# Hyperedge degrees taken from accumulating comparisons on VectorE instead of from products with ones, and the high parts of the second aggregation ahead of its low parts

## The reference, cut to what matters

```python
H = (adj != 0).astype(x.dtype)
w = adj.reshape(N, -1)[:, :C]
xw = jnp.einsum('ncd,hd->nch', x, W)
Dn = jnp.einsum('nce,ne->nc', H, w);  Dn = jnp.where(Dn > 0, 1.0 / Dn, 0.0)
Be = H.sum(axis=1);                   Be = jnp.where(Be > 0, 1.0 / Be, 0.0)
m = Be[:, :, None] * jnp.einsum('nce,nch->neh', H, xw)
out = Dn[:, :, None] * jnp.einsum('nce,neh->nch', H, m)
```

## Time and profile before

| | |
|---|---|
| median of three runs | 738.5 us (737.72 to 739.07) |
| the profiled execution, its own time | 737.89 us |
| its span, first to last instruction | 736.4 us |
| granted TensorE clock, mean | 0.987 |
| PE busy | 697.6 us (95%), 5573 products |
| DVE busy | 637.7 us (87%) |
| ACT busy | 495.6 us (67%) |
| POOL busy | 298.5 us (41%) |
| one graph in the steady loop | about 42.5 us |

### The profile page before, as it was taken

One profiled execution on the slowest core, in us unless ns is written; L12 is line 12 of the kernel. 1 busy time (PEld: TensorE's weight loads), 2 busy tenths in 40 slices (PEclk: granted clock), 3 DMA queues, 4 the chain that ended last, 5 costly groups with the idle time before them and its releaser, 6 DMA issues.

```text
span 736.4 us, 16435 instructions
## 1 busy us (share of the span) xinstructions
PE 697.6 (95%) x5573; PEld 486.5 (66%) x5573; DVE 637.7 (87%) x1569; ACT 495.6 (67%) x971; POOL 298.5 (41%) x685
## 2 busy tenths in 40 slices
PE   4787999999999999999999999999999999999983
PEld 2365595866758586776858577685957668595772
DVE  3887799889989898998989999898998989898676
ACT  4565858667595857668594866859486685957563
POOL 4142524245352524435352434436243543624233
PEclk9999999999999999999999999999999999999997
DMA  8447449376665839476573947556493756537312
GB/s 285 181 76 240 99 131 229 59 232 134 214 129 151 200 58 267 103 219 123 167 175 73 273 81 228 114 194 148 101 259 67 234 116 202 110 89 161 58 31 57
DMA packets 42591, 111.73 MB, mean 152 GB/s; under 512 B 4160, under 2 KB 5312, under 8 KB 42560
## 3 DMA queue, kind: packets, MB, share of 16 engines
q0 software_dynamic: 13536, 41.42, 31.8%
q1 hardware_dynamic: 29024, 69.92, 27.3%
HBM read 69.91 MB, written 16.25 MB: 117 GB/s over the span
## 4 chain that ended last, share of the span: by engine, by line
PE 86%; DVE 6%; ACT 3%; DMA 1%; issue 1%; POOL 1%; SPq 0%; POOLq 0%; DVEq 0%; ACTq 0%
PE bank L1278 16%; PE bank L1279 16%; PE bank L1280 16%; PE bank L1363 7%; PE bank L1364 7%; PE bank L1422 4%; PE bank L1423 4%; PE bank L1392 3%; PE bank L1332 3%; PE bank L1394 3%; PE bank L1380 2%; PE bank L1325 2%; DMA b1b<-b 1%; PE bank L1435 1%; PE bank L1410 1%
## 5 line engine op out<-in xcount | busy, mean ns | idle before, releaser
L1278 PE MATMUL bank<-xth,ewh 128*128 128x512 f16 (+1 forms) x272 | 101.0, 371 | 2.5 <-DVE ewl L794 2.5
L1279 PE MATMUL bank<-xtl,ewh 128*128 128x512 f16 (+1 forms) x272 | 101.0, 371 | 0.0
L1280 PE MATMUL bank<-xth,ewl 128*128 128x512 f16 (+1 forms) x272 | 100.8, 371 | 0.0
L519 ACT ACTIVATE silu<-bank,ebcol,ksc 128x512 f32<-128x512 f32 x120 | 90.5, 769 | 9.2 <-POOL comb L389 4.9
L1278 PE MATMUL bank<-w2h,hnth 128*128 128x256 f16 x256 | 70.3, 275 | 0.2 <-issue 0.2
L1279 PE MATMUL bank<-w2l,hnth 128*128 128x256 f16 x256 | 70.3, 275 | 0.0
L1280 PE MATMUL bank<-w2h,hntl 128*128 128x256 f16 x256 | 70.2, 274 | 0.0
L560 ACT ACTIVATE a1h<-bank,be 128x256 f16<-128x256 f32 x64 | 26.9, 470 | 55.7 <-PE bank L1423 52.5
L893 DVE SCALAR_TENSOR_TENSOR hntl<-bank,hnth 128x512 f16<-128x512 f32 x64 | 42.7, 687 | 23.5 <-ACT hnth L537 23.5
L666 ACT ACTIVATE uh<-bank,be 128x256 f16<-128x256 f32 x64 | 26.9, 471 | 53.7 <-PE bank L1364 53.7
L1422 PE MATMUL bank<-xsh,h 128*128 128x256 f16 x256 | 59.3, 280 | 1.1 <-DVE xsl L776 1.1
(11 more groups left out here) (260 smaller groups left out, 2124.9 us busy)
## 6 DMA issues: line engine op xcount, KB each, us to landing
adjin<-adj SPq DMA_DIRECT2D x16, 1024.0 KB, 5.3
adjtin<-adjt SPq DMA_DIRECT2D x16, 1024.0 KB, 7.9
xin<-x SPq DMA_DIRECT2D x16, 512.0 KB, 7.0
xb<-xn SPq DMA_DIRECT2D x16, 512.0 KB, 4.0
xb<-x POOLq DMA_DIRECT2D x16, 512.0 KB, 8.7
xb<-b POOLq DMA_DIRECT2D x16, 512.0 KB, 5.4
xb<-vadd POOLq DMA_DIRECT2D x16, 512.0 KB, 4.5
out<-x SPq DMA_DIRECT2D x15, 512.0 KB, 4.9
```

The source lines that it names most:

```text
L519: af(silu[:, i % 4, :], bank[E_BANK[i]][:, :], ACT.Silu, bias=ebcol[:, i:i + 1], scale=ksc[:, 2:3]).then_inc(silu_dn, 1)
L1278: mm(outp, lh, rh, start=first, stop=False)
L1279: mm(outp, lh, rl, start=False, stop=False)
L1280: return mm(outp, ll, rh, start=False, stop=last)
```

## The change

The degrees are no longer products. `prep_ht` makes `ht16` tile by tile, and each of the four comparisons also adds up its row into a column of `deg` (`accum_out`). The first two tiles are compared early, ahead of `hnt_part(g, 0)`, and the other two where all four were. `degrees` moves to the end of the body of the graph before, behind `prep_h`, and `be` gets two buffers. `dna` and `dnb` move from DVE to POOL (`scale_dn`), where they stand ahead of `prep_x`. In `a2_half` all products with `a1h` come first and wait for ACT only; `turned_x2(f, 0)` moves in between them and those with `a1l`. The semaphore counts follow.

```diff
@@ POOL
+            def scale_dn(g):
+                gp.wait_ge(d_step, 4 * g + 4)
+                tt(dna[:, :], dn[:, :], ksc[:, 0:1].to_broadcast([P, CT]), ALU.mult).then_inc(dn_scaled, 1)
+                tt(dnb[:, :], dn[:, :], ksc[:, 1:2].to_broadcast([P, CT]), ALU.mult).then_inc(dn_scaled, 1)
...
+                if conv:
+                    if not ffn:
+                        gp.wait_ge(b_scale, 1)
+                    scale_dn(g)
                 if prep and ffn:
                     prep_x(g + 1)
@@ DVE
-            def prep_ht(g, odd):
-                dve.wait_ge(adjt_in, 16 * g + 16)
-                TS(ht16[odd][:, :, :], adjtin[:, :, :], 0.0, None, ALU.not_equal).then_inc(ht_made, 1)
+            def prep_ht(g, odd, tiles=range(CT)):
+                if tiles[0] == 0:
+                    dve.wait_ge(adjt_in, 16 * g + 16)
+                for t in tiles:
+                    TS(ht16[odd][:, t, :], adjtin[:, t, :], 0.0, None, ALU.not_equal, ALU.add,
+                       accum_out=deg[:, t:t + 1]).then_inc(ht_made, 1)
...
-                dve.wait_ge(d_step, 6 * g + 4)
-                TS(dna[:, :], dn[:, :], ksc[:, 0:1], None, ALU.mult).then_inc(d_step, 1)
+                dve.wait_ge(d_step, 4 * g + 4)
...
-            def degrees(g):
-
-                dve.wait_ge(deg_rdy, g + 1)
-                TS(dmax[:, :], bank[DEG_BANK][:, DEG], 1.0, None, ALU.max).then_inc(be_max, 1)
+            def degrees(g, odd):
+
+                dve.wait_ge(ht_made, 4 * g + 4)
+                TS(dmax[:, :], deg[:, :], 1.0, None, ALU.max).then_inc(be_max, 1)
                 dve.wait_ge(be_max, g + 1)
-                v.reciprocal(be[:, :], dmax[:, :]).then_inc(be_dn, 1)
+                v.reciprocal(be[odd][:, :], dmax[:, :]).then_inc(be_dn, 1)
...
                     x1_half(f, 1, late)
-                if conv:
-                    degrees(g)
                 if ffn:
                     stats_x1(f, 1)
                 if conv:
                     if not ffn:
                         prep_ht(0, 0)
+                        degrees(0, 0)
...
-                    TS(dnb[:, :], dn[:, :], ksc[:, 1:2], None, ALU.mult).then_inc(d_step, 1)
...
                 if ffn:
                     combine(f, 1)
+                if prep:
+                    prep_ht(g + 1, 1 - odd, (0, 1))
                 if conv and ffn:
                     hnt_part(g, 0)
...
                 if prep:
-                    prep_ht(g + 1, 1 - odd)
+                    prep_ht(g + 1, 1 - odd, (2, 3))
...
                 if prep:
                     prep_h(g + 1)
+                    degrees(g + 1, 1 - odd)
@@ PE
-                pe.wait_ge(a1_lo, 4 * g + CG * half + CG)
+                def part(a, first, last):
+                    for d in range(KD):
+                        for k in range(CG * half, CG * half + CG):
+                            ins = mm(bank[A2_BANK[d]][:, :], a[:, k, P * d:P * d + P], ht16[odd][:, k, :],
+                                     start=(first and k == 0), stop=(last and k == CT - 1))
+                        if last and half == 1:
+                            ins.then_inc(a2_rdy, 1)
+
+                pe.wait_ge(a1_hi, 4 * g + CG * half + CG)
                 if half == 0 and ffn:
                     pe.wait_ge(u_lo, 4 * g)
                     pe.wait_ge(x1_dn, 4 * (g - 1) + 2)
...
+                part(a1h, True, False)
+                if ffn and half == 0:
+                    turned_x2(g - 1, 0)
+                pe.wait_ge(a1_lo, 4 * g + CG * half + CG)
+                part(a1l, False, True)
...
-                    for e in range(CT):
-                        for k in range(CT):
-                            ins = mm(bank[DEG_BANK][:, DEG][:, e:e + 1], h16[:, k, P * e:P * e + P], one16[:, :],
-                                     start=(k == 0), stop=(k == CT - 1))
-                    ins.then_inc(deg_rdy, 1)
-
...
-                if ffn:
-                    turned_x2(f, 0)
```

More of the change, by code:

```diff
@@ L128, in build @@
         xb = sb("xb", [P, CT, D], F32)
-        dmax, be = (sb(n, [P, CT], F32) for n in ("dmax", "be"))
+        deg, dmax = sb("deg", [P, CT], F32), sb("dmax", [P, CT], F32)
+        be = (sb("be_even", [P, CT], F32), sb("be_odd", [P, CT], F32))
         dsum, dclip, drec, dn, dna, dnb = (sb(n, [P, CT], F32) for n in ("dsum", "dclip", "drec", "dn", "dna", "dnb"))
@@ L203, in build @@
         a2_lo, v_lo, xt_lo, ct_lo, y_dn = (sem(n) for n in ("a2_lo", "v_lo", "xt_lo", "ct_lo", "y_dn"))
+        dn_scaled = sem("dn_scaled")
         comb_st, half_sum = sem("comb_st"), sem("half_sum")
@@ L306, in _ @@
             nc.gpsimd.memset(m16[:, :, :], 0.0).then_inc(tables, 1)
-            nc.gpsimd.memset(one16[:, :], 1.0).then_inc(tables, 1)
-            gp.wait_ge(tables, 13)
+            gp.wait_ge(tables, 12)
             for m in (ident16, ident):
@@ L572, in body @@
                 if conv:
-                    a1_part(act, g, 0)
+                    a1_part(act, g, odd, 0)
                 if ffn:
@@ L576, in body @@
                 if conv:
-                    a1_part(act, g, 1)
+                    a1_part(act, g, odd, 1)
                 if conv and not ffn:
@@ L821, in setup_mag_b @@
             def setup_mag_b():
-                dve.wait_ge(tables, 16)
+                dve.wait_ge(tables, 15)
                 dve.wait_ge(b_abs, KH + 1)
@@ L912, in y_part, with a1_part @@
                     ALU.mult, ALU.add).then_inc(y_dn, 1)
-            def a1_part(g, j):
+            def a1_part(g, odd, j):
                 dve.wait_ge(a1_hi, 4 * g + CG * j + CG)
                 for e in range(CG * j, CG * j + CG):
-                    STT(a1l[:, e, :], bank[A1_BANK[j]][:, D * (e % CG):D * (e % CG) + D], be[:, e:e + 1], a1h[:, e, :],
+                    STT(a1l[:, e, :], bank[A1_BANK[j]][:, D * (e % CG):D * (e % CG) + D], be[odd][:, e:e + 1], a1h[:, e, :],
                         ALU.mult, ALU.subtract).then_inc(a1_lo, 1)
@@ L983, in x1_half @@
                     dve.wait_ge(xb_dn, 16 * g + 16)
-                    dve.wait_ge(d_step, 6 * g + 6)
+                    dve.wait_ge(dn_scaled, 2 * g + 2)
                     if again:
@@ L1026, in body @@
                 if conv:
-                    a1_part(g, 0)
+                    a1_part(g, odd, 0)
                 if late:
@@ L1032, in body @@
                         setup_scale_a()
-                    a1_part(g, 1)
+                    a1_part(g, odd, 1)
                 if late:
@@ L1068, in body @@
                         d_vector(g)
-                    dve.wait_ge(d_step, 6 * g + 5)
+                    dve.wait_ge(dn_scaled, 2 * g + 1)
                     z_part(g, 0)
@@ L1389, in a2_half @@
                     pe.wait_ge(x1_dn, 4 * (g - 1) + 2)
-                for d in range(KD):
-                    for k in range(CG * half, CG * half + CG):
-                        mm(bank[A2_BANK[d]][:, :], a1h[:, k, P * d:P * d + P], ht16[odd][:, k, :],
-                           start=(k == 0), stop=False)
-                        ins = mm(bank[A2_BANK[d]][:, :], a1l[:, k, P * d:P * d + P], ht16[odd][:, k, :],
-                                 start=False, stop=(k == CT - 1))
-                    if half == 1:
-                        ins.then_inc(a2_rdy, 1)
+                part(a1h, True, False)
[3 more added lines that the diff above has]
+                part(a1l, False, True)
             def body(pe, g, odd, conv, ffn, late, prep):
@@ L1427, in body @@
                             turn_mags(a_mag, slice(W1, W1 + 1), 0, a_turn)
-                    pe.wait_ge(ht_made, g + 1)
+                    pe.wait_ge(ht_made, 4 * g + 4)
                     pe.wait_ge(w_cur, g + 1)
@@ L1608, in tail @@
                 last_out(1)
-            pe.wait_ge(tables, 18)
+            pe.wait_ge(tables, 17)
             steps(pe, body, tail)
```

24 lines of the change are left out of this document (11 added, 13 removed).

## The result

The changed kernel takes 733.79 us (median of six runs, 732.65 to 735.57) against 738.79 us for the kernel before in six runs; the ratio is 0.9931, with a 95% interval of 0.9908 to 0.9954. The forecast was 733.6 us, and 731.6 to 736.8 us. The profiled execution took 732.65 us with a span of 731.1 us, 5.3 us less than the span before.

What follows compares the result with a forecast made beforehand. PE's instruction list was taken to set the period from the second graph on; -5.7 us for the degree products and +0.8 us in the first two graphs gave -4.9, from 738.5 to 733.6 us, range 731.6 to 736.8 us.

Steps and rivals of the forecast that it cites:

- PE loses the degree products: On PE ahead of A1: 16 products leave its list, 0.41 us a graph over 14 graphs, 5.7 us.
- A comparison costs 0.65 us: On DVE: each accumulating comparison takes 0.65 us a tile, 2.6 us a graph instead of 1.13.
- The far bound (0.80): Upper cost of a comparison on DVE: the hntl distance of 0.60 plus an accumulator read of 0.20 us; total time 734.6 us.
- The early pair hides in the hole: On DVE ahead of hntl of tile 0: two comparisons, 1.3 us, fit an idle stretch of 1.45 us.
- ctl is next, with 0.10 us: If the early pair overran, ctl for out_product would be late; an overrun over 0.10 us a graph stalls PE.
- The late pair is hidden: On DVE ahead of ul: 1.3 us replaces 1.13, ul starts 0.17 us late, and nothing passes on to PE.
- Moved: degrees, dna and dnb at new places: a1l keeps 0.1 us, x2 ends 0.14 us late, no stall on PE.
- rival A: At a1l and x2: chains without slack give back half of the 0.41 us; 736.4 us; chance 0.16.
- B: Rival: the early pair overruns the hole, DVE bounds through ctl, out_product stalls each graph; up to 746.5 us; chance 0.08.
- The reorder of a2_half costs and brings nothing: Second aggregation on PE: x2 gets 0.86 us more, a2_rdy of the first bank comes 0.43 us later; both costed at nothing.
- The start, +0.8 us: First two graphs: early pair ahead of hntl +1.0, dna's trip to POOL +0.1, be off the chain -0.3 us.
- The rest, 0: Behind the first transposed_h of graph 15: a change of 0 us was forecast.

Runs made afterwards that it cites:

- e2_no_products: The kernel before with the 16 degree products left out and be made from a constant; 732.16 us, ratio 0.9918.
- e1_deg_first: The changed kernel with degrees one place earlier, ahead of prep_h and behind the second pair of comparisons; 733.15 us, ratio 0.9928 to the kernel before.
- the repeat: The changed kernel itself run once more, with no edit; 734.01 us, ratio 0.9945 to the kernel before.
- e8_pair_at_jump: The kernel before with two short, unused four-column DVE instructions behind prep_h at the end of each body; 739.88 us, ratio 1.0016.
- e7_dna_on_vector: The changed kernel with dna and dnb scaled on DVE again, at their old places; 734.12 us, ratio 0.9937 to the kernel before.
- e9_best: The changed kernel with degrees ahead of prep_h and, in graph 0, all four comparisons at the late place; 731.90 us, ratio 0.9911 to the kernel before.

## Why the prediction was right, and the step that failed

- *PE loses the degree products, 0.41 us a graph.* Right: 0.40 us with the products alone left out (e2_no_products), and 42.05 us in every body without a jump.
- *A comparison costs 0.65 us.* 0.61 us, at the 0.60 of the `hntl` row that I leaned on. The far bound (0.80) had the accumulator's read at its full length, but the next comparison starts with it.
- *The early pair hides in the hole; ctl is next, with 0.10 us.* Right in the place: the hole keeps 0.37 us, and an overrun of 0.235 us makes PE wait for `ctl`. The slack of 0.10 us was not confirmed: 0.06 us of the overrun comes through without a jump and 0.24 us behind one. The hole itself was misread, too: from 299.11 to 300.60 us are 1.49 us and not 1.45, so at 0.80 us a tile the overrun of 0.11 us would have been worth nearly nothing, not 0.7 us.
- *The late pair is hidden.* Right: PE never waits for `ul` in the loop; with all four comparisons there it does, by 0.55 us. "Even at 0.80 us a tile" was too much said: 0.47 us late against 0.41 us of idle time leaves 0.06.
- *Moved: "By `a1l` at 321.60 the sum on DVE is the same", and for x2 "No stall".* This is the step that failed. The sum of the instructions was the same, but the pair now stands ahead of the loop's jump, and the jump costs 0.60 us of DVE when nothing long runs in front of it. x2 was left with -0.14 us of slack, and the 0.60 us came on top; PE loses 0.25 us behind each of the five jumps back; without them, in e1_deg_first, the 14 periods are 1.06 us shorter. It is the outcome of rival A in kind (some of the 0.41 us lost at the chain that I had named, about a fifth where A had half), but by a mechanism that I did not have. The sign for A and B was a wait for x2 or `ctl` in every graph, and both came in every second one. `a1l`, for which I had expected an idle time of 0.1 us ahead of it, has none in the loop, and PE does not wait for it.
- *The reorder of a2_half costs and brings nothing.* Wrong by 1.5 us in this kernel: it hides a part of the jump, of which PE would otherwise lose 0.43 us and not 0.25. In the kernel without an exposed jump it is worth 0.03 us a graph: the four transposes take 0.43 us from their start to the next product behind 512-column products (279.78 to 280.21), and 0.47 us right behind the 4-column products of D (322.68 to 323.15 in the kernel before).
- *The start, +0.8 us.* +0.47 us. From the first transposes of graph 0 to those behind the wait for `hntl` it is 0.80 us longer (43.40 - 34.24 against 42.68 - 34.32), where I had +1.0; from there to graph 1 it is 0.25 us shorter, for `be`'s -0.3; what lies ahead is 0.08 us shorter. The idle time in PE's row went from 0.94 to only 1.35 us, and to 1.61 in the repeat, at the same delay.
- *The rest, 0.* -0.99 us in this pair of profiles, -0.37 us in the repeat. Up to the end of B3 (18.8 us behind the transposes) the two kernels run alike; the granted clock from 700 us to the end is 0.82 before and, from 696 us, 0.86 after. It is scatter, and in the sum it covered the term of the jump: -5.7 + 0.8 was -4.9, and it came as -4.78 + 0.47 - 0.99 = -5.3. Without the scatter it would have been -4.3. That the number fits as well as it does is luck.

## What to carry to other kernels

Where one engine's list sets the period, count what leaves the list from the distance between starts, and pay for what moves to the other engine out of a named hole; the same work some 13 us later cost 0.75 us a graph. Look at which instruction stands in front of a loop's jump: a long one hides the jump, and two short ones expose it, so an edit that moves small work to the end of a body is not neutral, though no unit of work is added. And beside hand-overs with little slack, a delay on an engine that has 10% idle time is the bottleneck's delay.

## What the runs showed of the hardware that I had not expected

- A jump back to a loop's start leaves DVE idle for 0.58 to 0.64 us behind two instructions on four columns, and for nothing behind a comparison of 1.22 us (changed, e8_pair_at_jump, e1_deg_first). At the loop's entry it is 0.30 to 0.34 us, at its exit 0.18 us.
- A comparison of 512 columns with an accumulator has a distance of 0.61 us, four of them 2.4 us, where one comparison of 2048 columns without it has 1.13 us: a little over twice the time for the same columns.
- 0.6 us of VectorE work in graph 0 cost 2.7 us by the medians (1.8 by the ratios). In the profile TensorE's longer wait there (1.94 us) was followed by some 3 us at the lower clock level, worth 1.65 us; e7_dna_on_vector has the same behind a wait of 2.00 us without that work, and e9_best behind one of 2.06 us elsewhere.
- POOL's wait for the landing of one DMA in graph 4 was 3.05 us in the changed kernel and 4.49 us in e7_dna_on_vector; the roots for ACT stand behind it in POOL's queue, and that one period grew by over 1 us.
